# Attention scores of a head pair: two heads' steps, one after the other, become one step that alternates between two PSUM banks

## The reference, cut to what matters

```
scores[h, w] = Q[h, w] @ K[h, w-1 .. w].T      # 128 queries x 256 keys, 64 features
scores += mask                                  # 0 or -1e30
probs  = exp(scores - max) ; out = (probs @ V) / sum
```

## Time and profile before

| what | value |
|---|---|
| time, median of 3 runs | 5062.9 us (5062.59 to 5064.84) |
| span of the profiled execution | 5060.7 us |
| TensorE busy | 4509.6 us, 89% |
| VectorE busy | 4181.3 us, 83% |
| ScalarE busy | 3166.3 us, 63% |
| GpSimd busy | 2078.6 us, 41% |

### The profile page before, as it was taken

How to read it: one execution, slowest core, us unless ns; L and a number is a source line. 1 busy time by engine, 2 the same in 40 slices (tenths; PEclk the granted TensorE clock), 3 DMA queues, 4 the chain that set the end, 5 groups by cost and what they waited for, 6 DMA issues and landing times.

```text
span 5060.7 us, 75398 instructions
## 1 busy us (share of the span) xinstructions
PE 4509.6 (89%) x20080; PEld 2766.1 (55%) x20208; DVE 4181.3 (83%) x8946; ACT 3166.3 (63%) x6063; POOL 2078.6 (41%) x2033
## 2 busy tenths in 40 slices
PE   5679899898998989899998998989889998998989
PEld 3345555564555655555564555655555564555655
DVE  5689798888979889798888979889798888979853
ACT  2447666675766757666675766757666675666745
POOL 2234344443434444344443434444344443434423
PEclk8779999999999999999999999999999999999979
DMA  4001101111101101101111101101101111101100
GB/s 120 15 26 28 29 25 30 28 30 29 26 26 28 34 22 28 29 25 30 28 29 29 26 26 27 35 21 29 29 25 30 27 30 29 26 25 28 35 19 20
DMA packets 144530, 149.37 MB, mean 30 GB/s; under 512 B 27748, under 2 KB 107932, under 8 KB 143960
## 3 DMA queue, kind: packets, MB, share of 16 engines
q1 hardware_dynamic: 144088, 144.19, 10.9%
HBM read 22.45 MB, written 4.19 MB: 5 GB/s over the span
## 4 chain that ended last, share of the span: by engine, by line
PE 51%; DVE 27%; issue 14%; ACT 4%; POOL 1%; SPq 1%; DVEq 1%; DMA 0%; ACTq 0%; POOLq 0%
PE bT L1302 8%; DVE acc L952 8%; DVE tmp L952 6%; PE bA L1174 5%; PE bC L1359 5%; PE bU L1352 5%; PE bG L1345 4%; PE bA L1264 4%; PE bT L1314 4%; PE bT L1158 3%; DVE tmp L814 3%; PE bT L1287 2%; PE bA L1255 2%; DVE hu L1139 2%; PE bT L1327 2%
## 5 line engine op out<-in xcount | busy, mean ns | idle before, releaser
L644 POOL TENSOR_TENSOR s_h<-s_h,ge 128x512 f32<-128x512 f32 x512 | 730.2, 1426 | 1303.7 <-ACT ge L654 1052.9
L776 ACT ACTIVATE s_h<-bG 128x512 f32<-128x512 f32 x528 | 314.0, 595 | 709.9 <-DVE hu L1139 421.6
L952 DVE TENSOR_TENSOR acc<-acc,tmp 128x512 f32<-128x512 f32 x768 | 696.9, 914 | 4.2
L603 POOL TENSOR_TENSOR veA<-mvA,epsT 128x2 f32<-128x2 f32 x290 | 112.9, 389 | 1315.8 <-DVE mvA L807 1315.8
L1359 PE MATMUL bC<-hu,w_d 128*128 128x512 f32 x1056 | 582.3, 634 | 10.0 <-DVE hu L1139 9.6
L952 DVE TENSOR_TENSOR tmp<-comps 128x512 f32<-128x512 f32 x768 | 582.1, 766 | 5.8
L1302 PE MATMUL bT<-Kk,Q 64*128 64x256 f32 (+1 forms) x2048 | 545.5, 388 | 31.2 <-DVE y L1121 7.3
L753 ACT ACTIVATE probs<-bT,nmax 128x256 f32<-128x256 f32 x1024 | 413.6, 474 | 229.7 <-DVE nmax L1100 225.8
L1100 DVE TENSOR_REDUCE nmax<-bT 128x2 f32<-128x512 f32 x512 | 350.2, 685 | 194.4 <-PE bT L1302 192.3
L1314 PEld LDWEIGHTS bT<-V,probsT 128*128 128x128 f32 x3584 | 433.4, 194 | 79.6 <-issue 36.0
L1139 DVE TENSOR_TENSOR hu<-bU,s_h 128x512 f32<-128x512 f32 x528 | 360.8, 683 | 108.7 <-PE bU L1352 74.5
(11 more groups left out here) (201 smaller groups left out, 9650.8 us busy)
## 6 DMA issues: line engine op xcount, KB each, us to landing
rot<-raw SPq DMA_DIRECT2D x1024, 64.0 KB, 2.0
comps<-comps SPq DMA_DIRECT2D x384, 120.0 KB
x_ld<-in_L_attn_x SPq DMA_DIRECT2D x66, 128.0 KB, 2.2
comps<-comps SPq DMA_DIRECT2D x384, 8.0 KB
out<-O SPq DMA_DIRECT2D x16, 256.0 KB, 2.7
w_a<-in_L_attn_W_qkv SPq DMA_DIRECT2D x1, 1536.0 KB, 14.8
w_fc<-in_L_attn_fc_w SPq DMA_DIRECT2D x1, 1024.0 KB, 8.3
w_g<-in_L_ffn_w_gate SPq DMA_DIRECT2D x1, 1024.0 KB, 5.9
```

The lines of the kernel that those rows point to most:

```text
L644: nc.gpsimd.tensor_tensor(s_h[:, :], s_h[:, :], ge[:, :], ALU.mult).then_inc(weighed, 1)
L776: nc.scalar.activation(s_h[:, :], bG[:, :], ACT.Silu).then_inc(silu, 1)
L952: V_.tensor_tensor(dst, i0, i1, op).then_inc(ham[h], 1)
```

## The change

`S p 0` and `S p 1` are now issued together where `S p 0` stood, and `S p 2` and `S p 3` together where `S p 2` stood. Where `S p 1` and `S p 3` stood, TensorE does nothing. A pair begins with the waits and the mask matmul of its first head, then those of its second head; then the score matmuls follow in the order head 0, head 1 for the first window, head 0, head 1 for the second. The bank, the partitions and the result of each step are as before, and so are the orders of the other engines. `ORDER` is not touched.

```diff
+                def scores(*t):
+                    p, first_w = t[1], t[2] // 2 * 2
+                    both = [("S", p, first_w + h) for h in range(2)]
+                    if t[2] == 0:
+                        pe.wait_ge(roped, r.b * len(ROPE_ORDER) + (ROPE_ORDER.index(("k", p)) + 2))
+                    for s in both:
+                        t_begin(pe, r, s)
+                        mm(t_bank(s)[:, :], identb[:, :], maskb[:, first_w * WIN:first_w * WIN + S], start=True, stop=False)
+                    for k in range(2):
+                        w = first_w + k
+                        n = min(w, 1) + 1
+                        for h, s in enumerate(both):
+                            f = slice(h * DH, (h + 1) * DH)
+                            ins = mm(t_bank(s)[:, ((k + 1) * 2 - n) * WIN:(k + 1) * 2 * WIN], Q[f, w * WIN:(w + 1) * WIN],
+                                     Kk[f, (w + 1 - n) * WIN:(w + 1) * WIN], start=False, stop=k == 1)
+                            if k == 1:
+                                ins.then_inc(t_full, 1)
+
                 def t_part(*t):
+                    if t[0] == "S":
+                        if t[2] % 2 == 0:
+                            scores(*t)
+                        return
...
-                    if t[0] == "S":
-                        first_w, h = t[2] // 2 * 2, t[2] % 2
-                        f = slice(h * DH, (h + 1) * DH)
-                        if t[2] == 0:
-                            pe.wait_ge(roped, r.b * len(ROPE_ORDER) + (ROPE_ORDER.index(("k", t[1])) + 2))
-                        mm(b[:, :], identb[:, :], maskb[:, first_w * WIN:first_w * WIN + S], start=True, stop=False)
-                        for k in range(2):
-                            w = first_w + k
-                            n = min(w, 1) + 1
-                            ins = mm(b[:, ((k + 1) * 2 - n) * WIN:(k + 1) * 2 * WIN], Q[f, w * WIN:(w + 1) * WIN],
-                                     Kk[f, (w + 1 - n) * WIN:(w + 1) * WIN], start=False, stop=k == 1)
```

## The result

The changed kernel takes 5420.1 us (median of 4 runs, 5418.4 to 5426.5) against 5062.9 before: 357 us or 7.1% slower, ratio 1.0706 with a 95% interval of 1.0691 to 1.0721. The forecast was 5290, with 5415 as the upper end, so the sign and the kind of the loss were right and its size was not. The profiled execution has a span of 5420.0 us.

What follows compares the result with a forecast made beforehand. TensorE and VectorE in turns were taken as the bound. Costs of 19.1, 3.5, 6.4 and 2.0 less savings of 6.1 and 4.2 gave 20.7 us a round; 70% over 16 rounds added 230: about 5290 us, range 5125 to 5415.

Steps and rivals of the forecast that it cites:

- What bounds the kernel: Loop round: TensorE and VectorE alternate on the chain, neither with much room; TensorE idle only 27 of 303.8 us.
- Mode switches: Sixteen joined pairs a round each save one trip into and out of 64-row form, 0.38 us: 6.1 us.
- Overlap: Joined pairs' two heads' score passes may run side by side: 0 to 8.5 us saved a round, 4.2 taken.
- The second pair waits: At S p 2's place, S p 3 waits for S p 0's exponentials to free its bank: 19.1 us a round.
- The first pair waits: At S p 0's place, pairs 2 to 6, S p 1's bank awaits the copy into `raw`: 3.5 us a round.
- S p 3 in front of other work: In six pairs a projection or expert step, and S p 2's maximum, wait 1.07 us more: 6.4 us a round.
- Clock: TensorE passes run at half clock after long waits, as in pairs 0 and 1: 2 us a round, bounds 0 and 5.
- I let 70% through: Of the net 20.7 us a round on TensorE, 70% reaches the end, 14.4 us; idle time absorbs the rest.

Runs made afterwards that it cites:

- its control: Kernel before the change, with only the maximum and exponentials of S p 0 reading a constant SBUF tile instead of the bank: 5064.0 us, ratio 1.0001.
- The fills: Changed kernel with the mask written extra times into S p 2's already owned bank during TensorE's longest waits: 5285.7 us, ratio 1.0440.
- the run without the wait: Changed kernel, but S p 3 need not wait for S p 0's exponentials; S p 0's maximum and exponentials read a constant tile: 5040.7 us, ratio 0.9958.
- the waits alone: Kernel before the change, nothing joined or moved; only the bank waits of S p 1 and S p 3 also stand at S p 0's and S p 2's places: 5549.3 us.

## Why the prediction was wrong, step by step

- **What bounds the kernel: right.** TensorE and VectorE in turns with little room. That there was so little room counts against a later step.
- **Mode switches: about 0.30 for the 0.38 I took.** Joined steps have one round trip instead of two. In pair 4 it is 2801.27 to 2802.64, less 0.21 for the mask and 0.86 for the passes: 0.30, the same as in the earlier trace rows. The 0.1 for weights that are not loaded ahead was in the 0.29 already, as far as the rows show it, so the term is nearer 4.8 us a round than 6.1.
- **Overlap: too small.** I took 4.2 us a round of a supposed most of 8.5, with three of eight passes side by side. Both matmuls of a window start together, so four of eight are: 4 x 0.215 = 0.86 us in a second pair and 0.64 in a first, 12 us a round.
- **The second pair waits: right in place, a little high in size.** 248.5 / 16 = 15.5 us a round measured, 19.1 forecast; pair 1 had 4.9 for 5.2, pair 0 2.2 for 2.8, pair 2 2.5 for 2.7, pair 5 2.5 for 3.0. Pair 4, for which I had 1.0, had none; why was not followed up.
- **The first pair waits: right.** 55.6 / 15 = 3.7 for 3.5.
- **S p 3 in front of other work, 6.4 us: not confirmed.** Without the bank wait the joined pair stands in front of the same work, and the kernel is 23 us faster than its control. There it is outweighed by the savings; its own size wasn't isolated.
- **Clock, 2 us a round with 5 as bound: this step failed.** The fills gave back 134 us, 8 us a round, and the busy time against the run without the wait is 162 us longer, 10 us a round. I had seen one stretch of 3.4 us at half clock behind a wait of 4.04, and counted it for pairs 0 and 1 alone. Shorter waits brought it too, in pairs 2 and 5 after 2.50 us and in pair 7 after 2.19, though not in pair 0 after 2.20. Time at half clock rose by 364 us in the run. Pair 2 of the changed kernel, and the busy times and the clock there, in the columns of the earlier trace rows:

```profile
2729.42 0.61 PE L1278 MATMUL bT<-maskb,identb 128*128 128x512 bf16 x1 [2.50 <-ACT probs L753]
2729.95 2.08 PE L1284 MATMUL bT<-Kk,Q 64*128 64x256 f32 x8
...
2729.00:2736.00 7.00, 6.58 (x28) 5.22 (x29) 1.99 (x4) 1.93 (x5) 0.00 (x0) 0.52 0.22 57
```

  The eight passes alone take 1 us more here than in pair 4, and the projection behind them is slow as well. At 2 to 3 us for each of four such pairs the term would have been about right.
- **"I let 70% through": wrong, and this step failed too.** It takes one share for the sum, costs less savings. The costs came through in full: with the waits alone, 301 us of standing and 190 of slower work made up nearly all of the 497 us between the two profiled executions. Of the savings a tenth came through, 23 of 207 us. TensorE's 27 idle microseconds absorbed nothing; VectorE was held by the same stall (its waits at the maximum rose from 192.3 to 511.5 us in that run). With the terms as measured the forecast's sum would have been smaller than 20.7, about 10 us a round (19 with the 6.4 for S p 3), so that even at 100% it could not give the 22 measured (357 / 16).
- The two errors met the missed overlap with the other sign. Without the clock's part the kernel is at 5286; the forecast without its clock term (2 x 0.7 x 16 = 22) was 5268. That the rest agrees so well is partly luck: an overlap taken too small made the forecast too high, and a share of 70% for the costs made it too low.

Not tried: moving ScalarE's and VectorE's steps in `ORDER` so that S p 0's exponentials come sooner. The parts of the clock's loss that the fills did not reach were not separated either.

## What to carry to other kernels

Before joining two steps that rotate through a few buffers, count the buffers: with three banks the fourth step's wait is for the first, and moving it forward makes it wait for a whole round trip through two other engines. Price a wait on TensorE twice, once for standing and once for the slow clock behind it. Do not set it off against time saved on TensorE at one rate: where another engine takes turns with it, the wait arrives in full and most of the saving may not. And where no better order is at hand, harmless matmuls into a bank already owned are cheaper than standing still. Join steps whose banks are freed by something else, even if they are less natural partners.

## What the runs showed of the hardware

- Two fp32 matmuls of 64 partitions each, one on partitions 0 to 63 and one on 64 to 127 and into different banks, run fully side by side: eight passes in 0.93 us against 1.57 with both on the same partitions. The order of issue, alternating or head by head, made no difference (5416 and 5420 us).
- Between the start of the mask matmul of 128 rows and that of the first one of 64 rows there are 0.31 us; mask matmuls behind each other start 0.215 us apart (11 in 2662.41 to 2664.78).
- In the round read here the clock was at its lower level, 1.2 GHz, for the passes behind waits at the mask of 2.19, 2.50, 2.50 and 4.90 us, and at 2.4 GHz behind one of 2.20. Behind two waits in front of `hart`, of 1.53 and 1.93 us, it was at the lower level too, so in this kernel the length of a wait alone does not tell it. Mask matmuls in the waits at the mask left the scores behind them at 2.4 GHz in all eight pairs and made the kernel 134 us faster in one case and, with the waits in front of `hart` and of O's transposes, 25 us in another.
